# Expert part of a fused GNN and mixture-of-experts kernel: W1 held in the array from a fixed buffer, h made transposed, gathers placed behind the scatters

## The chip, the cores and the metric

One core of one Trainium2 chip. The metric is the device time of one execution in microseconds; a kernel's time is the median of its runs.

## The reference, cut to what matters

625 nodes with 256 features pass a three-level edge convolution (20,000 edges) and are added to the input. What follows is the part that the change touches: a layer norm, a gate that picks 2 of 8 experts for each node, and for each picked expert a two-layer network.

```python
gate_scores = x @ Wg + bg
_, idx = jax.lax.top_k(gate_scores, K)                    # K = 2 of E = 8
h = jax.nn.gelu(jnp.einsum('td,edh->teh', xf, W1) + b1[None], approximate=False)   # D = 256, H = 512
y = jnp.einsum('teh,ehd->ted', h, W2) + b2[None]
out = jnp.einsum('ted,te->td', y, mf)                     # sum over the picked experts
x = x + out
```

All of it is float32.

## The kernel before

The convolution takes the first 117 us of the span and is not touched. The expert part works on the picked pairs only. The 1250 (node, expert) pairs are sorted by expert into tiles of 128 slots; each tile belongs to one expert (`owner_i`), and there are at least `FIXED` = 10 tiles and at most 17. The trace has 13: ten in code that is written out, two in one turn of a loop over pairs of tiles (`Fori`), and one behind an `If`. Unused slots are sent to spare rows behind the output.

In what follows tile s is counted from 0. For each tile:

- its x rows: tiles 0 and 1 are gathered by one-hot matmuls (`gather` on PE, lines 1529 to 1540); from tile 2 on by an indirect DMA of POOL from `x2_rows` in DRAM (`gather`, line 587) into one of twelve buffers `xg`, then transposed on PE (`transpose_x`, line 1552) and copied by ACT to `xt` (line 787, tiles 0 and 1: line 799);
- `up` (line 1545): for each half k of the 256 features, the transposed x is the stationary operand and 512 columns of W1 move; two float32 matmuls, which the trace shows as four instructions. h comes out with slots on partitions;
- DVE adds b1 (line 1203), ACT applies gelu (line 792), PE transposes h in four pieces (line 1558), ACT copies them to `h_t` (line 796);
- `down` (line 1564): four float32 matmuls (eight instructions) with a piece of `h_t` held and 256 columns of W2 moving;
- DVE adds b2 and writes y to one of four buffers `y_sb` (line 1207);
- POOL adds the rows of y to the output in DRAM with an accumulating indirect DMA (`scatter`, line 593).

A node has two experts, so two scatters can hit the same output row. POOL therefore waits for `scattered`, that is for the landing of scatter s - 1, before it issues scatter s. POOL's queue is in this order: the gathers of tiles 2 to 9, then for s = 0 to 9 scatter s and, for s below 4, the gather of tile 10 + s. In the loop it waits for the landing, copies the row numbers of the tile to a fixed column (`row_put`, line 613), waits for that copy, counts `pool_turn` up (line 616), scatters, copies the next fetch's row numbers (`row_get`, line 624), counts up again and gathers.

PE's order in step s is: transpose h of tile s, up of tile s + 1, transpose x of tile s + 2, down of tile s. Ahead of the expert tiles PE runs filler matmuls on the identity (`keep_busy`, line 1272: float32, 128 columns held, 128 moving; each shows as two instructions).

SP loads b1 as eight broadcasts to 128 partitions and b2 as one (lines 479 to 482), behind the copy of x1 to the output; ACT's queue stores the normed rows to `x2_rows` (lines 780 and 781), which POOL's first gather waits for (line 582), as it does for `row_of` (`rows_ready`, line 1231).

Of the kernel before, what the change touches and what calls it, by code (L numbers as in the profile page):

```python
# [8 lines left out]
D = 256  # L9
LEVELS = 3  # L10
EXPERTS = 8
# [73 lines left out]
FIXED = -(-2 * NODES // P)  # L85
assert FIXED % 4 == 2 and SPARE + P <= NPAD + P


def build(nc, x, src, dst, W, B, Wf, bf, Wg, bg, W1, b1, W2, b2, out):
# [8 lines left out]
    with ctx:  # L98
# [83 lines left out]
        b1_bc = sb("b1_bc", [P, EXPERTS, HID], f32, ffn)  # L182
# [48 lines left out]
        h_pre = sb("h_pre", [P, 2, HID], f32, ffn)  # L231
        h_act = sb("h_act", [P, 2, HID], f32, ffn)
        h_t = sb("h_t", [P, HC, P], f32, ffn)
# [105 lines left out]
        pre_ready = sem("pre_ready")  # L339
        act_ready = sem("act_ready")  # L340
        t_done = sem("t_done")
        h_t_ready = sem("h_t_ready")
        down_done = sem("down_done")
# [50 lines left out]
        def first_experts(kind):  # L394

            _, ids = nc.values_load_multi_w_load_instructions(
                owner_i[0:1, 0:FIXED + 1], engines=(kind,), min_val=0, max_val=EXPERTS - 1,
                skip_runtime_bounds_check_because="a count of at most EXPERTS, cut to EXPERTS - 1 just above")
            return ids
# [47 lines left out]
        def _(sp):  # L447
# [31 lines left out]
            for e in range(EXPERTS):  # L479
                sp.dma_start(b1_bc[:, e, :], b1[e].partition_broadcast(P)).then_inc(ffn_b_in, 16)  # L480
# [7 lines left out]
        def _(pool):  # L488
# [121 lines left out]

            def late_scatter(s, h, n_late):
                pool.wait_ge(scattered, s * 16)
                pool.tensor_copy(row_put[:, h:h + 1], row_of[:, ds(s, 1)]).then_inc(put_taken, 1)
                pool.wait_ge(put_taken, n_late)
                pool.wait_ge(y_ready, s + 1)
                pool.sem_inc(pool_turn, 1)
                scatter(2 + h, row_put[:, h:h + 1])

            with pool.Fori(0, more) as p:
# [18 lines left out]
        def _(act):  # L638
# [155 lines left out]
            def h_transposed(s):  # L794
                act.wait_ge(t_done, s + 1)
                act.copy(h_t[:], bank[2].rearrange("p (k s) -> p k s", k=HC)).then_inc(h_t_ready, 1)  # L796
# [3 lines left out]
            gelu(0, 0)  # L800
            gelu(1, 1)
            for s in range(FIXED):
                h_transposed(s)
                x_transposed(s + 2, s % 2)
                if s:
                    gelu(s + 1, (s + 1) % 2)
            act.wait_ge(experts_ready, 2)
            more = pairs(act)
            with act.Fori(0, more) as p:
                for h in range(2):  # L810
                    s = p * 2 + (FIXED + h)
                    h_transposed(s)
                    x_transposed(s + 2, h)
                    gelu(s + 1, 1 - h)
            with act.If(odd_tile(act) > 0):
                h_transposed(more * 2 + FIXED)
# [3 lines left out]
        def _(dve):  # L820
# [366 lines left out]
            dve.tensor_copy(owner_i[:], owner[:])  # L1187
# [13 lines left out]
            def add_b1(s, h, e):  # L1201
                dve.wait_ge(up_done, s + 1)
                dve.tensor_tensor(h_pre[:, h, :], up_bank(h)[:, :], b1_bc[:, ds(e, 1), :], ALU.add).then_inc(pre_ready, 1)  # L1203
# [29 lines left out]
            dve.wait_ge(ffn_b_in, 16 * (EXPERTS + 1))  # L1233
            e_of = first_experts(mybir.EngineType.DVE)
            add_b1(0, 0, e_of[0])
            add_b1(1, 1, e_of[1])
            for s in range(FIXED):
                if s:
# [391 lines left out]
```

## Time and profile before

| | us |
|---|---|
| median of three runs | 209.98 (209.79 to 211.39) |
| profiled execution, its own time | 211.53 |
| its span, first to last instruction | 209.7 |
| expert tiles, first up to the last scatter's start | 138.24 to 202.88 |

The span is what the trace shows; 1.83 us of the profiled execution's time lie outside it. Rows give a start in us from the span's start, a length, the engine and the line. A PE row's length includes the way through the array, so that neighbouring matmuls overlap in the list; their starts tell the pace. An entry in square brackets is the idle time ahead of an instruction and who ended it. The granted clock of TensorE is at its full level from 63 us until the last expert tile's matmuls at about 195 us.

### The profile page before, as it was taken

What the parts mean: (1) busy time and instruction counts of PE and PEld (TensorE: products, weight loads), DVE (VectorE), ACT (ScalarE), POOL (GpSimd) and SP (SyncE); (2) the same over time, 40 slices, a digit from 0 to 9 for tenths busy, and PEclk for the clock granted to TensorE, in tenths of its full rate; (3) what the DMA queues carried; (4) which work ended last, traced back from release to release, by engine and by line L of the source; (5) the groups of instructions that cost most, each with busy time, mean ns of one, the idle gap of its engine ahead of it and who ended that gap; (6) DMA issues with size and microseconds to landing.
All of it is one profiled execution on the core that took longest, in us unless ns stands there. A gap on an engine that the chain in (4) does not pass through costs nothing.

```text
span 209.7 us, 3186 instructions
## 1 busy us (share of the span) xinstructions
PE 163.0 (78%) x1033; PEld 134.7 (64%) x1034; DVE 101.5 (48%) x268; ACT 71.9 (34%) x196; POOL 61.4 (29%) x85
## 2 busy tenths in 40 slices
PE   0351175858999999999999979997999999997100
PEld 0240165647998779998899969965677667665100
DVE  5499699797009465414624878922232223222000
ACT  4283586563004116202520076023334434343000
POOL 7006000000960039003000200027864732243660
PEclk9999999995599999999999999999999999999755
DMA  5500022000014000699990079903344332322332
GB/s 151 166 15 0 0 90 66 0 2 3 2 17 140 3 5 0 157 377 366 366 367 28 18 211 289 367 18 102 102 65 81 54 30 32 41 25 27 53 50 25
DMA packets 16121, 20.50 MB, mean 98 GB/s; under 512 B 1842, under 2 KB 12452, under 8 KB 15972
## 3 DMA queue, kind: packets, MB, share of 16 engines
q1 hardware_dynamic: 12580, 15.75, 23.2%
q0 software_dynamic: 2544, 3.54, 10.3%
q10 hardware_dynamic: 976, 0.93, 1.4%
q8 instruction: 13, 0.21, 0.4%
q14 instruction: 8, 0.07, 0.1%
HBM read 16.96 MB, written 3.26 MB: 96 GB/s over the span
## 4 chain that ended last, share of the span: by engine, by line
PE 45%; DMA 20%; DVE 18%; issue 8%; POOL 3%; ACT 2%; ACTq 1%; POOLq 0%; DVEq 0%
DMA out_rows<-y_sb,row_of 14%; PE bank L1412 5%; DVE hot_lo L874 4%; DMA out_rows<-y_sb,row_put 4%; PE cnt_ps L1412 3%; PE bank L1265 3%; PE cnt_ps L1272 3%; PE bank L1267 3%; PE bank L1266 3%; PE g_ps L1265 3%; DVE hot_key L877 2%; PE g_ps L1266 2%; PE g_ps L1267 2%; DMA dst_chunk<-in_dst 2%; POOL out_rows L593 2%
## 5 line engine op out<-in xcount | busy, mean ns | idle before, releaser
L1564 PE MATMUL cnt_ps<-w_sb,h_t 128*128 x104 | 24.8, 381 | 1.7 <-ACT h_t L796 1.7
L1313 PE MATMUL bank<-hot_key,hot_lo 125*128 125x45 bf16 (+4 forms) x80 | 8.4, 244 | 18.7 <-DVE hot_key L877 9.1
L1564 PEld LDWEIGHTS cnt_ps<-w_sb,h_t 128*128 128x128 f32 x104 | 18.7, 190 | 4.2 <-issue 2.2
L593 POOL DMA_INDIRECT out_rows<-y_sb,row_of x10 | 15.7, 1574 | 18.3 <-DMA out_rows<-y_sb,row_of 13.0
L1313 PEld LDWEIGHTS bank<-hot_key,hot_lo 125*128 125x128 bf16 x80 | 5.4, 123 | 21.5 <-DVE hot_key L877 14.4
L587 POOL DMA_INDIRECT xg<-x_rows,row_of x12 | 11.8, 983 | 22.8 <-DMA x_rows<-x_f 19.4
L1207 DVE TENSOR_TENSOR y_sb<-cnt_ps,b_bc 128x256 f32<-128x256 f32 x13 | 5.5, 424 | 22.8 <-PE cnt_ps L1564 12.0
L874 DVE TENSOR_TENSOR hot_lo<-iota_lo,edge_rel 125x1024 bf16<-125x1024 int16 x20 | 13.6, 681 | 2.1 <-PE g_ps L1313 2.0
L1545 PE MATMUL bank<-w_sb,xt 128*128 x28 | 13.3, 596 | 0.0
L1272 PE MATMUL cnt_ps<-ident 128*128 128x128 f32 x100 | 12.0, 277 | 0.0
L557 POOL IOTA key_tables<- 128x720 int16 x1 | 2.2, 2244 | 32.9 <-DVE a_hi L960 32.9
L796 ACT COPY h_t<-cnt_ps 128x512 f32<-128x512 f32 x13 | 7.6, 585 | 11.8 <-PE cnt_ps L1558 11.8
L1272 PEld LDWEIGHTS cnt_ps<-ident 128*128 128x128 f32 x100 | 11.5, 192 | 0.0
L1545 PE MATMUL g_ps<-w_sb,xt 128*128 x24 | 11.3, 593 | 0.0
L792 ACT ACTIVATE h_act<-h_pre 128x512 f32<-128x512 f32 x13 | 8.2, 630 | 7.6 <-DVE h_pre L1203 7.6
L1412 PE MATMUL bank<-a_hi,ys_hi 128*128 128x384 f32 x30 | 10.2, 341 | 0.5 <-issue 0.5
L1203 DVE TENSOR_TENSOR h_pre<-bank,b_bc 128x512 f32<-128x512 f32 x7 | 4.8, 691 | 11.7 <-PE bank L1545 11.7
L1412 PE MATMUL bank<-a_hi,ys_lo 128*128 128x384 f32 x30 | 10.1, 338 | 0.0
L787 ACT COPY xt<-bank 128x256 f32<-128x256 f32 x12 | 4.5, 372 | 14.9 <-PE bank L1552 14.9
L1265 PE MATMUL g_ps<-w_hi,ht_hi 128*128 128x256 f32 x30 | 9.3, 310 | 0.0
L1266 PE MATMUL g_ps<-w_lo,ht_hi 128*128 128x256 f32 x30 | 9.1, 304 | 0.0
L1267 PE MATMUL g_ps<-w_hi,ht_lo 128*128 128x256 f32 x30 | 9.1, 303 | 0.0
(270 smaller groups left out, 427.9 us busy)
## 6 DMA issues: line engine op xcount, KB each, us to landing
w_sb<-in_L_ffn_W SPq DMA_DIRECT2D x16, 512.0 KB, 9.5
b_bc<-in_L_ffn_b SPq DMA_DIRECT2D x8, 256.0 KB, 5.6
w_stage<-in_L_gnn_W SPq DMA_DIRECT2D x3, 512.0 KB, 4.1
w_stage<-in_L_gnn_Wf SPq DMA_DIRECT2D x4, 256.0 KB, 4.4
b_bc<-in_L_ffn_b SPq DMA_DIRECT2D x1, 1024.0 KB, 12.3
x_rows<-x_f ACTq DMA_DIRECT2D x1, 640.0 KB, 8.4
x_sb<-in_x SPq DMA_DIRECT2D x1, 512.0 KB
out_rows<-x_sb SPq DMA_DIRECT2D x1, 512.0 KB
```

The source lines that it names most:

```text
L587: pool.indirect_dma_start(out=xg[:, b, :], out_offset=None, in_=x2_rows, in_offset=bass.IndirectOffsetOnAxis(ap=rows, axis=0)).then_inc(x_ ...
L593: pool.indirect_dma_start(out=out, out_offset=bass.IndirectOffsetOnAxis(ap=rows, axis=0), in_=y_sb[:, b, :], in_offset=None, compute_op=AL ...
L792: act.activation(h_act[:, h, :], h_pre[:, h, :], ACT.Gelu).then_inc(act_ready, 1)
L874: dve.tensor_tensor(hot_lo[:, u % RING:u % RING + 2, :, :], iota_lo[0:EP].unsqueeze(1).broadcast_to((EP, 2, P, CT)), rel[:, 0].unsqueeze(2 ...
L1265: pe.matmul(out_, lh, rh, start=first, stop=False, skip_group_check=True)
L1266: pe.matmul(out_, lh, rl, start=False, stop=False, skip_group_check=True)
L1267: return pe.matmul(out_, ll, rh, start=False, stop=last, skip_group_check=True)
L1272: pe.matmul(bank[free][:, 0:P], ident[:], ident[:], start=True, stop=True)
L1313: last = pe.matmul(pane(k), hot_lo[:, u % RING, :, i], hot_keys(u)[:, 0, :, i], start=i == i0, stop=i == i0 + n_i - 1, skip_group_check=True)
L1412: step = pe.matmul(z_bank(i), y[:, u, m], a_t[:, u, cols], start=first and u == 0 and y is y_parts[0], stop=last and u == NT - 1 and y is ...
L1545: last = pe.matmul(up_bank(h)[:, :], xt[:, k, h * P:(h + 1) * P], w1_sb[:, ds(e, 1), k, :], start=k == 0, stop=k == KC - 1)
L1564: last = pe.matmul(bank[3][:, 0:D], h_t[:, k, :], w2_sb[:, ds(e, 1), k, :], start=k == 0, stop=k == HC - 1)
```

## The change

- **W1.** Each tile's W1 (256 x 512) and b1 are copied from where all experts lie to one of two fixed buffers, `w1_now` and `b1_now`: for tiles 0 and 1 by ACT ahead of the copy of their x, from tile 2 on by DVE (`take_w1`), one step and more ahead of use.
- **up** holds 128 columns of `w1_now` and moves the 128 columns of x: eight float32 matmuls of 128 columns. h comes out transposed, so that the four transposes on PE, the copy of `h_t` on ACT and the addition of b1 on DVE go. gelu reads PSUM in four pieces, each with its b1 column as bias, and writes `h_t`, which has two buffers now.
- **b1** is loaded once, as 32 rows of 128, transposed on PE behind the filler matmuls and ahead of the gather, and copied by ACT. The eight broadcasts go.
- **PE's order** in step s is: wait for xt of tile s + 1, transpose x of tile s + 2, up of tile s + 1, down of tile s. In step 0 it is down of tile 0, then transpose x of tile 2.
- **POOL's order**: gathers of tiles 2 to 6, then for s = 0 to 9 scatter s and, for s below 7, the gather of tile 7 + s. In the loop the copy to `row_put` for the next scatter stands behind the present one.

```diff
+AHEAD = 7
...
-            for e in range(EXPERTS):
-                sp.dma_start(b1_bc[:, e, :], b1[e].partition_broadcast(P)).then_inc(ffn_b_in, 16)
+            sp.dma_start(b1_rows[:], b1.rearrange("e (c p) -> (e c) p", c=HC)).then_inc(b1_in, 16)
...
-            for s in range(2, FIXED):
+            for s in range(2, AHEAD):
                 gather(s, row_of[:, s:s + 1])
             pool.wait_ge(x1_stored, 48)
             for s in range(FIXED):
+                pool.wait_ge(y_ready, s + 1)
                 if s:
                     pool.wait_ge(scattered, s * 16)
-                pool.wait_ge(y_ready, s + 1)
                 scatter(s % 4, row_of[:, s:s + 1])
-                if s < 4:
-                    gather((FIXED + s) % (FIXED + 2), row_of[:, FIXED + s:FIXED + s + 1])
+                if AHEAD + s < FIXED + 4:
+                    gather((AHEAD + s) % (FIXED + 2), row_of[:, AHEAD + s:AHEAD + s + 1])
...
+            def next_put(s, h):
+                pool.tensor_copy(row_put[:, h:h + 1], row_of[:, ds(s, 1)]).then_inc(put_taken, 1)
             def late_scatter(s, h, n_late):
-                pool.wait_ge(scattered, s * 16)
-                pool.tensor_copy(row_put[:, h:h + 1], row_of[:, ds(s, 1)]).then_inc(put_taken, 1)
                 pool.wait_ge(put_taken, n_late)
                 pool.wait_ge(y_ready, s + 1)
+                pool.wait_ge(scattered, s * 16)
                 pool.sem_inc(pool_turn, 1)
                 scatter(2 + h, row_put[:, h:h + 1])
...
                     late_scatter(s, h, p * 2 + (h + 1))
+                    next_put(s + 1, 1 - h)
                     pool.wait_ge(x_t_done, s + 1)
...
             def gelu(s, h):
-                act.wait_ge(pre_ready, s + 1)
-                act.activation(h_act[:, h, :], h_pre[:, h, :], ACT.Gelu).then_inc(act_ready, 1)
+                act.wait_ge(up_done, s + 1)
+                act.wait_ge(w1_now_ready, s + 1)
+                for c in range(HC):
+                    last = act.activation(h_t[:, h, c, :], up_bank(h)[:, c * P:(c + 1) * P], ACT.Gelu,
+                                          bias=b1_now[:, h, c:c + 1])
+                last.then_inc(h_t_ready, 1)
+            act.wait_ge(b1_t_ps, 1)
+            act.copy(b1_t[:], bank[2][:, 0:EXPERTS * HC].rearrange("p (e c) -> p e c", e=EXPERTS))\
+                .then_inc(b1_t_ready, 1)
+            act.wait_ge(b1_t_ready, 1)
+            act.wait_ge(owner_ready, 1)
+            e_of = first_experts(mybir.EngineType.Activation, 2)
+            for h in range(2):
+                act.copy(b1_now[:, h, :], b1_t[:, ds(e_of[h], 1), :])
+                act.copy(w1_now[:, h, :, :], w1_sb[:, ds(e_of[h], 1), :, :]).then_inc(w1_now_ready, 1)
             act.wait_ge(gathered, 1)
             act.copy(xt[:], gather_ps()).then_inc(xt_ready, 2)
             gelu(0, 0)
+            x_transposed(2, 0)
             gelu(1, 1)
-            for s in range(FIXED):
-                h_transposed(s)
+            for s in range(1, FIXED):
                 x_transposed(s + 2, s % 2)
-                if s:
-                    gelu(s + 1, (s + 1) % 2)
+                gelu(s + 1, (s + 1) % 2)
...
+            def take_w1(s, h, e):
+                dve.wait_ge(up_done, s - 1)
+                dve.wait_ge(h_t_ready, s - 1)
+                dve.tensor_copy(b1_now[:, h, :], b1_t[:, ds(e, 1), :])
+                dve.tensor_copy(w1_now[:, h, :, :], w1_sb[:, ds(e, 1), :, :]).then_inc(w1_now_ready, 1)
...
             for s in range(FIXED):
-                if s:
-                    dve.wait_ge(act_ready, s)
-                    add_b1(s + 1, (s + 1) % 2, e_of[s + 1])
+                take_w1(s + 2, s % 2, e_of[s + 2])
                 if s >= 4:
                     dve.wait_ge(scattered, 16 * (s - 3))
                 add_b2(s, s % 4, e_of[s])
...
-            def up(s, h, e):
+            def up(s, h):
                 pe.wait_ge(xt_ready, s + 1)
-                for k in range(KC):
-                    last = pe.matmul(up_bank(h)[:, :], xt[:, k, h * P:(h + 1) * P], w1_sb[:, ds(e, 1), k, :],
-                                     start=k == 0, stop=k == KC - 1)
+                pe.wait_ge(w1_now_ready, s + 1)
+                for c in range(HC):
+                    for k in range(KC):
+                        last = pe.matmul(up_bank(h)[:, c * P:(c + 1) * P], w1_now[:, h, k, c * P:(c + 1) * P],
+                                         xt[:, k, h * P:(h + 1) * P], start=k == 0, stop=k == KC - 1)
                 last.then_inc(up_done, 1)
...
             keep_busy(WARM_GATHER)
+            pe.wait_ge(b1_in, 16)
+            pe.transpose(bank[2][:, 0:EXPERTS * HC], b1_rows[:], ident[0:EXPERTS * HC, 0:EXPERTS * HC])\
+                .then_inc(b1_t_ps, 1)
             pe.wait_ge(x2_lo_done, NT)
             gather()
...
+            up(0, 0)
+            up(1, 1)
+            down(0, 0, e_of[0])
+            transpose_x(2, 1)
+            for s in range(1, FIXED):
+                pe.wait_ge(xt_ready, s + 2)
                 transpose_x((s + 2) % (FIXED + 2), 1)
-                if s:
-                    pe.wait_ge(y_ready, s)
-                down(s, e_of[s])
+                pe.wait_ge(h_t_ready, s)
+                up(s + 1, (s + 1) % 2)
+                pe.wait_ge(y_ready, s)
+                down(s, s % 2, e_of[s])
```

The loop and the odd tile are changed in the same way on PE, ACT and DVE.

## Rows read from the trace of the kernel before

**Rows 1.** The page, part 4: lines on the chain that ended last

```profile
DMA out_rows<-y_sb,row_of 14%; PE bank L1412 5%; DVE hot_lo L874 4%; DMA out_rows<-y_sb,row_put 4%; PE cnt_ps L1412 3%; PE bank L1265 3%; PE cnt_ps L1272 3%; PE bank L1267 3%; PE bank L1266 3%; PE g_ps L1265 3%; DVE hot_key L877 2%; PE g_ps L1266 2%; PE g_ps L1267 2%; DMA dst_chunk<-in_dst 2%; POOL out_rows L593 2%
```

**Rows 2.** Timeline, POOL alone, 134 to 210 us: start, length, line, [idle before <-releaser]

```profile
140.18 1.19 POOL L587 DMA_INDIRECT xg<-x_rows,row_of  x1 [19.43 <-DMA x_rows<-x_f]
...
145.44 0.94 POOL L587 DMA_INDIRECT xg<-x_rows,row_of  x1 [0.30 <-issue]
...
149.19 0.95 POOL L587 DMA_INDIRECT xg<-x_rows,row_of  x1 [0.30 <-issue]
150.44 1.63 POOL L593 DMA_INDIRECT out_rows<-y_sb,row_of  x1 [0.30 <-issue]
...
187.80 1.55 POOL L593 DMA_INDIRECT out_rows<-y_sb,row_of  x1 [2.46 <-DMA out_rows<-y_sb,row_of]
...
192.82 1.56 POOL L593 DMA_INDIRECT out_rows<-y_sb,row_put  x1 [0.88 <-DVE y_sb L1207]
...
195.43 1.03 POOL L587 DMA_INDIRECT xg<-x_rows,row_get  x1 [0.83 <-POOL row_get L624]
...
202.88 1.58 POOL L593 DMA_INDIRECT out_rows<-y_sb,row_put  x1 [0.88 <-POOL row_put L613]
```

**Rows 3.** The chain of waits in order of time: start, length, what

```profile
150.44 3.72 DMA out_rows<-y_sb,row_of
154.16 0.27 issue
...
171.31 4.15 issue
...
192.07 0.55 issue
```

**Rows 4.** Timeline, all engines, one tile: start, length, engine, line

```profile
154.04 0.60 PE L1558 MATMUL cnt_ps<-ident,h_act 128*128 128x128 f32 x4
...
154.47 1.88 PE L1545 MATMUL bank<-w_sb,xt 128*128 x4
...
156.41 1.89 PE L1564 MATMUL cnt_ps<-w_sb,h_t 128*128 x8
...
158.14 0.60 PE L1558 MATMUL cnt_ps<-ident,h_act 128*128 128x128 f32 x4
```

**Rows 5.** Timeline, from the gathered tiles to y of tile 0

```profile
137.46 0.59 ACT L799 COPY xt<-bank 128x512 f32<-128x512 f32 x1 [6.74 <-PE bank L1538]
...
138.24 1.96 PE L1545 MATMUL bank<-w_sb,xt 128*128 x4
...
138.69 0.18 DVE L1231 SCALAR_TENSOR_TENSOR row_of<-bank,unused 128x20 int32<-128x20 f32 x1
...
144.03 1.96 PE L1564 MATMUL cnt_ps<-w_sb,h_t 128*128 x8 [0.47 <-ACT h_t L796]
...
146.14 0.43 DVE L1207 TENSOR_TENSOR y_sb<-cnt_ps,b_bc 128x256 f32<-128x256 f32 x1 [3.39 <-PE cnt_ps L1564]
```

**Rows 6.** Timeline, the filler matmuls ahead of the gather

```profile
129.41 5.60 PE L1272 MATMUL cnt_ps<-ident 128*128 128x128 f32 x48
```

**Rows 7.** Groups by line and shape, ScalarE: busy, mean ns of one

```profile
L689 ACT CAST w_hi<-w_stage 128x512 fp32r<-128x512 f32 x3 | 1.7, 615 | 5.4 <-DVE w_stage L913 5.4
...
L678 ACT COPY a_f<-g_ps 128x95 f32 x4 | 1.0, 242 | 0.0
```

**Rows 8.** Line 389: a register load of one value, ns min/median/max

```profile
L389 ACTq TENSOR_LOAD <-pairs_i x1: 413/413/413, 181.9 to 181.9; - x1
```

**Rows 9.** Line 781, the second store of x_rows: us from issue to landing

```profile
DMA to landing us min/median/max: 10.8/10.8/10.8
```

**Rows 10.** The page, part 6: the b1 loads, KB each, us to landing

```profile
b_bc<-in_L_ffn_b SPq DMA_DIRECT2D x8, 256.0 KB, 5.6
```

**Rows 11.** Groups by line and shape, VectorE: busy, mean ns of one

```profile
L874 DVE TENSOR_TENSOR hot_lo<-iota_lo,edge_rel 125x1024 bf16<-125x1024 int16 x20 | 13.6, 681 | 2.1 <-PE g_ps L1313 2.0
...
L1216 DVE TENSOR_TENSOR hot_place<-iota_p,pos_f 128x1280 fp32r<-128x1280 f32 x1 | 1.5, 1481 | 0.0
```

More of the change, by code:

```diff
@@ L338, in build @@
         up_done = sem("up_done")
-        pre_ready = sem("pre_ready")
-        act_ready = sem("act_ready")
-        t_done = sem("t_done")
         h_t_ready = sem("h_t_ready")
+        b1_in = sem("b1_in")
+        b1_t_ps = sem("b1_t_ps")
+        b1_t_ready = sem("b1_t_ready")
+        owner_ready = sem("owner_ready")
+        w1_now_ready = sem("w1_now_ready")
         down_done = sem("down_done")
@@ L392, in odd_tile, with first_experts @@
             return eng.value_load(pairs_i[0:1, 1:2], min_val=0, max_val=1)
-        def first_experts(kind):
+        def first_experts(kind, n):
             _, ids = nc.values_load_multi_w_load_instructions(
-                owner_i[0:1, 0:FIXED + 1], engines=(kind,), min_val=0, max_val=EXPERTS - 1,
+                owner_i[0:1, 0:n], engines=(kind,), min_val=0, max_val=EXPERTS - 1,
                 skip_runtime_bounds_check_because="a count of at most EXPERTS, cut to EXPERTS - 1 just above")
@@ L1186, in _ @@
             mark(dve.scalar_tensor_tensor(in_tile[:], from_tile[:], float(P), from_tile[:], ALU.is_le, ALU.mult))
[L1187 removed]
+            dve.tensor_copy(owner_i[:], owner[:]).then_inc(owner_ready, 1)
             wait_marked()
@@ L1232, in _ @@
             dve.wait_ge(experts_ready, 2)
[L1233 to L1236, printed above, removed]
+            dve.wait_ge(ffn_b_in, 16)
+            e_of = first_experts(mybir.EngineType.DVE, FIXED + 2)
+            dve.wait_ge(b1_t_ready, 1)
             for s in range(FIXED):
-                if s:
-                    dve.wait_ge(act_ready, s)
-                    add_b1(s + 1, (s + 1) % 2, e_of[s + 1])
+                take_w1(s + 2, s % 2, e_of[s + 2])
                 if s >= 4:
@@ L1247, in _ @@
                     s = p * 2 + (FIXED + h)
-                    e_up = expert_of(dve, s + 1)
+                    e_up = expert_of(dve, s + 2)
                     e_down = expert_of(dve, s)
-                    dve.wait_ge(act_ready, s)
-                    add_b1(s + 1, 1 - h, e_up)
+                    take_w1(s + 2, h, e_up)
                     dve.wait_ge(scattered, s * 16 - 16)
@@ L1553, in transpose_x, with down @@
                 last.then_inc(x_t_done, 1)
-            def transpose_h(s, h):
-                pe.wait_ge(act_ready, s + 1)
-                for k in range(HC):
-                    last = pe.transpose(bank[2][:, k * P:(k + 1) * P], h_act[:, h, k * P:(k + 1) * P], ident[:])
-                last.then_inc(t_done, 1)
-            def down(s, e):
+            def down(s, h, e):
                 pe.wait_ge(h_t_ready, s + 1)
                 for k in range(HC):
-                    last = pe.matmul(bank[3][:, 0:D], h_t[:, k, :], w2_sb[:, ds(e, 1), k, :], start=k == 0,
+                    last = pe.matmul(bank[3][:, 0:D], h_t[:, h, k, :], w2_sb[:, ds(e, 1), k, :], start=k == 0,
                                      stop=k == HC - 1)
@@ L1578, in _ @@
             pe.wait_ge(experts_ready, 2)
[L1579 to L1585 removed]
+            e_of = first_experts(mybir.EngineType.PE, FIXED)
+            up(0, 0)
[4 more added lines that the diff above has]
+                pe.wait_ge(xt_ready, s + 2)
                 transpose_x((s + 2) % (FIXED + 2), 1)
[L1587 to L1589 removed]
+                pe.wait_ge(h_t_ready, s)
+                up(s + 1, (s + 1) % 2)
+                pe.wait_ge(y_ready, s)
+                down(s, s % 2, e_of[s])
             more = pairs(pe)
```

37 lines of the change are left out of this document (11 added, 26 removed).

## The prediction

> **What bounds the kernel now.** I read the chain that ended last first. Its largest part is the landing of scatters, 14% and 4% of the span [rows 1]; all of PE's `up` and `down` together do not appear among its leading lines. Then POOL's own timeline [rows 2]: eight gathers from 140.18, and right behind them scatter 0 at 150.44. From there scatters follow one another: 3.72 us from the start of a scatter to its landing, 0.27 until the next one starts [rows 3]. Ten scatters from 150.44 to 187.80 are 9 intervals of 37.36 us, 4.15 on average (one of them 4.9, with a late landing [rows 3]); then three in the loop and the `If`, at 192.82 and 202.88 the first and last, 5.0 apart [rows 2]. Behind the last start come 6.82 us to the span's end. So the end is the start of scatter 0, plus nine intervals, plus three long ones, plus 6.82.
>
> Then the same stretch on PE [rows 4]: PE is full, one tile from 154.04 to 158.14, 4.10 us. The two pipelines run at nearly the same pace, but y of tile 0 is ready at 146.57 [rows 5], four microseconds before its scatter, and this lead is kept. PE is busy without being the bound; POOL's queue is. A change is worth what it does to the start of the scatter chain and to its intervals.
>
> **The steady tile.** PE loses the four transposes of h, 0.43 (154.04 to 154.47, with the pace of the next instruction) and gets the new `up`. The old one takes 4 instructions of 512 columns: 156.41 less 154.47 is 1.94, of which two transposes of x take about 0.23 (half of the four of h), so 1.71. The new one is 16 instructions of 128 columns with a load each. That shape is in the trace: the filler on the identity, 48 in 5.60 us, 0.117 each with the loads beside it [rows 6], so 16 x 0.117 = 1.87. `down` stays, 158.14 less 156.41 = 1.73. A tile costs PE 0.23 + 1.87 + 1.73 = 3.83 in place of 4.10. Since the scatters need 4.0 to 4.15 a tile, these 0.27 become slack and buy nothing at the end. For PE to become the bound it would have to lose 0.3 a tile.
>
> ACT and DVE have the room: ACT goes from three pieces a tile to the copy of x and four short gelus (at about 0.3 each, below), DVE from one addition of 512 columns to a copy of 1024. w1 of tile s + 2 is copied right behind y of tile s - 1, and used one step later, so PE doesn't see it. `take_w1` waits for gelu of tile s, and behind it on DVE stands only b2 of tile s, which is needed two microseconds later. The ring of four y buffers doesn't bind: y leads the scatter by little more than one tile. The gathers behind scatters stand in the 2.1 us in which POOL only waits for a landing; scatters 0 to 3 had one already, at intervals no longer than the later ones. Gather 7 starts at 148 and tile 7 is transposed near 160.
>
> **The start: POOL's side.** Three gathers fewer ahead of scatter 0: 149.19 to 150.44 is one, 1.25, so 3.75. The first gather now starts at 140.18; `row_of` is ready at 138.69 + 0.18 = 138.87 [rows 5]. What came last by the profile is the store of x_rows, which took 10.8 us to land [rows 9], beside eight b1 broadcasts of 256 KB [rows 10]. These 2 MB go, and the store should land well before 138. Then the first gather waits for `row_of`: 138.87 + 0.1 for the b1 transpose that now stands on PE ahead of it + 0.27 from release to start [rows 3] = 139.25, 0.9 earlier. The bounds of this are 0 and 0.93; I take the whole. Five gathers: the fifth starts 5.26 behind the first, the next instruction 1.25 later [rows 2]; scatter 0 could start at 139.25 + 6.51 = 145.8.
>
> **The start: y's side.** Now ACT has work ahead of the copy of x. The b1 transpose can't run before the filler's end at 135.0 [rows 6], so: copy of b1 0.24 (like 95 columns, 0.242 [rows 7]), register load 0.41 for one value [rows 8] plus its decoding, about 0.75 for two, then two rounds of a short copy of 0.2 and one of 1024 columns. 512 columns take 0.615 and 95 take 0.242 [rows 7], 0.9 ns a column, so about 1.05. 135.1 + 0.24 + 0.75 + 2.5 = 138.6, where the copy of x had started at 137.46 [rows 5]: 1.1 us late. up of tile 0 starts at 139.35 in place of 138.24; up 0 and up 1 are 3.74, so down of tile 0 can start at 143.1. gelu of tile 0 is four pieces of 0.24 (PSUM, 95 columns) to 0.35, 1.2 in all, from 141.4 to 142.6: hidden behind up 1. Before, down had to wait for b1, gelu, transpose and copy, and started at 144.03; y was ready 2.54 later. Now y is ready at 145.6, and scatter 0 starts at 145.8: both sides meet. One stall is new: in step 1 PE waits for the copy of tile 2's x right behind its transpose, about 0.9 with latency and the copy's 0.4. y of tile 1: 143.1 + 1.73 + 0.9 + 3.83 + 0.17 + 0.45 = 150.2, so scatter 1 starts at 150.3 and not at 145.8 + 3.99 = 149.8. From y of tile 2 on (154.0 against 154.3) the chain of landings leads. Before, scatter 1 started at 154.43, so the chain is **4.1 us** earlier (3.7 if the first gather doesn't move).
>
> **The late scatters.** Before, each had between landing and start: 0.2 for addresses, the copy to `row_put` 0.19, and 0.7 to 0.85 behind the count of `pool_turn` (0.55 of it the row of [rows 3]), 1.24 in all. The copy and its wait move behind the previous scatter; the count stays. I take 0.85, a gain of 0.4 for each. In the loop another thing comes near: a gather ended 3.64 behind its scatter's start (195.43 + 1.03 against 192.82 [rows 2]), and with one more copy of about 0.2 ahead of it 3.85, as late as the landing. So 0.4, 0.35 and 0.4, **1.15** in all. Bounds: 0 (the count and the fuller queue eat it) and 2.0 (only 0.27 remains, and POOL's queue binds in the loop).
>
> **Sum.** 4.1 + 1.15 = 5.25 us off the profiled execution of 211.53, and since everything outside the stretch is the same, off the median: 209.98 - 5.25 = **204.7**. Around it: 3.7 + 0 gives 206.3, 4.1 + 2.0 gives 203.9, and 0.6 more where the late landing (4.9 for 4.1) doesn't come again, 203.3.
>
> **Rivals.** *First: DVE's copy holds POOL up.* DVE now copies 1024 float32 columns from SBUF to SBUF in each tile, and it starts right behind y, that is at the very time at which POOL makes a scatter's descriptors (1.57 us in each interval). The rows before show POOL's scatters at 1.55 to 1.63 whether DVE adds beside them or rests [rows 2], but those additions read PSUM; no copy of this kind is there. If such a copy stops POOL while it runs, with L its length, a scatter is delayed by L if the copy falls into it and by L/2 if it starts inside a copy: (1.57 L + L²/2) / 4.05 for random phases. DVE's 1024 columns took 0.68 at 16 bits, and 1280 of float32 took 1.48, which gives 1.22 for 1024 [rows 11]. With 0.68 the price is 0.32 a scatter, 4.2 for 13, 208.9; with 1.22 it is 0.66, 8.5, **213.2**, slower than before. It turns slower where a scatter pays over 0.4, a copy of about 0.83. The upper end needs the plain rate and a complete stop. Gathers that it hits have slack, so I set its middle at 208. Chance 0.26.
>
> The Trainium skill (SBUF — State Buffer, Who interferes with whom) says just that: a float32 copy inside SBUF runs in a mode that takes the ports which DVE shares with GpSimd, and descriptor generation stands still until the copy ends. Its page VectorE: DVE Perf Modes (The perf-mode tier table) gives such a copy twice the plain rate; an estimate from its 1227 ns for 2048 columns is 0.69 us for 1024. By that rule the low end of this rival holds; no row of the trace before can show it.
>
> *Second: only the queue's order pays.* The first gather doesn't move (3.7 in place of 4.1) and the late turns keep their 5.0: 206.3. For it: nothing in the trace shows what 0.55 us behind the count are. Chance 0.13.
>
> *Third: the loads aren't hidden.* If each of up's 16 loads (0.19) stood alone because their addresses change, up would take 3.04, a tile 5.0, and y of tile 12 would come at 206, 213. Against it: [rows 6] has the same load before each matmul at 0.117. Chance 0.03.
>
> **How the numbers follow.** Forecast 0.58 (203.3 to 206.3), then 0.26, 0.13 and 0.03. The range is 203.2 to 208.7, which leaves out the upper part of the first rival and the third. One per cent, 2.1 us, is about what a measurement can tell here: faster is the forecast, the second rival and a part of the first (0.07), 0.78; within 1% most of the rest of it, 0.13; slower 0.09.
>
> **What would show it.** Right: first gather near 139.3, scatter 0 near 145.8 with five gathers ahead, intervals of 4.0 to 4.15, late ones of 4.6, PE at 3.8 a tile with growing lead of y over the scatters, 16 instructions of `up` at 0.117. The first rival shows as scatters longer than 1.6 us, or landings over 3.85, where a copy of DVE lies beside them. Wrong would be: y of tile 0 later than 146, intervals that follow y, or a first gather that still starts behind 140.

## The result, and the profile after

| | before | after |
|---|---|---|
| median, us | 209.88 (209.62 to 211.39, 4 runs) | 212.44 (211.68 to 212.83, 4 runs) |
| profiled execution | 211.53 | 212.52 |
| its span | 209.7 | 210.3 |

The ratio is 1.010, 95% interval 1.006 to 1.014: about 1% slower, where 204.7 us were forecast. Some executions of any of these kernels take over 1.5% longer than its fastest; medians are over all runs, ratios and intervals leave those out. POOL's timeline of the changed kernel, with the columns of [rows 2]:

```profile
140.96 1.19 POOL L590 DMA_INDIRECT xg<-x_rows,row_of  x1 [19.79 <-issue]
...
146.44 0.95 POOL L590 DMA_INDIRECT xg<-x_rows,row_of  x1 [0.30 <-issue]
147.69 1.71 POOL L596 DMA_INDIRECT out_rows<-y_sb,row_of  x1 [0.30 <-issue]
...
152.41 1.59 POOL L596 DMA_INDIRECT out_rows<-y_sb,row_of  x1 [1.50 <-DMA out_rows<-y_sb,row_of]
...
189.67 1.93 POOL L596 DMA_INDIRECT out_rows<-y_sb,row_of  x1 [3.07 <-DVE y_sb L1224]
...
194.52 1.57 POOL L596 DMA_INDIRECT out_rows<-y_sb,row_put  x1 [2.72 <-DVE y_sb L1224]
...
199.06 1.57 POOL L596 DMA_INDIRECT out_rows<-y_sb,row_put  x1 [0.78 <-DMA out_rows<-y_sb,row_put]
...
203.64 1.56 POOL L596 DMA_INDIRECT out_rows<-y_sb,row_put  x1 [0.82 <-DMA out_rows<-y_sb,row_put]
```

(The profile names DVE as the releaser of the scatter at 189.67, but y of tile 9 had been ready for 9.6 us by then; what came last was the landing of scatter 8, at 188.92 in the chain.)

Scatter 0 is 2.75 us earlier than before, and the last one 0.76 later. What lies between can be read from the rows alone: 189.67 less 147.69 is 41.98 us for nine intervals, 4.66 each, against 37.36 and 4.15 in [rows 2]. The chain of waits says what each interval gained. Its first three lines are the first gather's:

```profile
139.67 0.03 issue
139.70 0.02 POOLq L586
139.71 1.24 issue
...
165.64 0.03 issue
165.67 0.02 POOLq L606
165.68 0.75 issue
166.43 3.76 DMA out_rows<-y_sb,row_of
170.19 0.02 issue
```

In [rows 3] 0.27 us lie between a landing and the next scatter. Here it is 0.02, then an instruction of 0.02 on POOL's queue, line 606, then 0.75. Line 606 is `pool.wait_ge(scattered, s * 16)`. The line's own view:

```profile
L606 POOLq EVENT_SEMAPHORE  x9: 17/17/17, 151.6 to 188.9; - x9
```

The wait for the landing has become an instruction of its own (a lone wait, in what follows), nine times. In the kernel before it left no record; there the wait for y (line 603) had one, and it passed microseconds ahead of time. The edit that swaps the two waits stands in the diff; in the changed kernel the landing is the later of the two each time.

The conv part ahead is unchanged, but the first filler matmul starts at another time in each trace, from 127.45 to 130.98 us over fifteen traces. So most times below are counted from the start of the row `x48` of the fillers ([rows 6], 129.41 before, 129.82 after):

| us behind the fillers' start | before | after |
|---|---|---|
| `row_of` ready | 9.46 | 9.84 |
| first gather of POOL | 10.77 | 11.14 |
| y of tile 0 | 17.16 | 15.53 |
| scatter 0 | 21.03 | 17.87 |
| scatter 9 | 58.39 | 59.85 |
| last scatter | 73.47 | 73.82 |

From one event to the next: first gather +0.37, gathers -3.53, nine intervals +4.62, late scatters -1.11; sum +0.35. The 1.0 us between the profiled executions is these 0.35, 0.41 of the fillers' start and 0.2 behind the last scatter's start and outside the span. The medians are 2.6 apart; the experiments come back to that.

PE and DVE do in a tile what was forecast. A tile of the changed kernel on PE, with its DVE rows:

```profile
153.12 0.38 PE L1567 MATMUL bank<-ident,xg 128*128 128x128 f32 x2
...
153.34 1.95 PE L1560 MATMUL bank<-xt,w_now 128*128 128x128 f32 x16
153.43 0.42 DVE L1224 TENSOR_TENSOR y_sb<-cnt_ps,b_bc 128x256 f32<-128x256 f32 x1 [2.64 <-PE cnt_ps L1573]
...
153.84 0.69 DVE L1220 COPY w_now<-w_sb 128x1024 f32 x1
...
155.13 1.89 PE L1573 MATMUL cnt_ps<-w_sb,h_t 128*128 x8
...
156.86 0.38 PE L1567 MATMUL bank<-ident,xg 128*128 128x128 f32 x2
```

3.74 us a tile (153.12 to 156.86), and 1.79 from the start of `up` (L1560) to that of `down` (L1573): 0.112 for each of the 16 instructions with its load. The copy of W1 takes 0.69 here.

### The profile page after: what moved, and what is told of

Its sections match the earlier page's. It is cut to its first block, busy times and chain, and to the rows that moved or that the text cites. A ratio compares the mean times of both kernels' runs of the same rounds, so it can differ in the third digit from the quotient of the medians.

```text
span 210.3 us, 3448 instructions
## 1 busy us (share of the span) xinstructions
PE 161.5 (77%) x1138; PEld 145.2 (69%) x1139; DVE 101.4 (48%) x279; ACT 73.2 (35%) x227; POOL 63.6 (30%) x85
## 4 chain that ended last, share of the span: by engine, by line
PE 50%; DMA 19%; DVE 18%; issue 6%; POOL 3%; ACT 1%; ACTq 1%; POOLq 0%; DVEq 0%
DMA out_rows<-y_sb,row_of 13%; PE bank L1425 5%; DVE hot_lo L888 4%; PE cnt_ps L1425 3%; PE cnt_ps L1573 3%; PE bank L1278 3%; PE cnt_ps L1285 3%; PE bank L1280 3%; PE bank L1279 3%; PE g_ps L1278 3%; PE g_ps L1280 2%; DVE hot_key L891 2%; PE g_ps L1279 2%; DMA dst_chunk<-in_dst 2%; DMA out_rows<-y_sb,row_put 2%
## 5 line engine op out<-in xcount | busy, mean ns | idle before, releaser
L1573 PE MATMUL cnt_ps<-w_sb,h_t 128*128 x104 | 27.7, 414 | 7.0 <-DVE y_sb L1224 4.5
L1573 PEld LDWEIGHTS cnt_ps<-w_sb,h_t 128*128 128x128 f32 x104 | 20.4, 207 | 10.5 <-issue 7.9
L596 POOL DMA_INDIRECT out_rows<-y_sb,row_of x10 | 16.7, 1672 | 17.5 <-DMA out_rows<-y_sb,row_of 10.7
L590 POOL DMA_INDIRECT xg<-x_rows,row_of x12 | 13.1, 1090 | 23.1 <-issue 23.1
L1560 PE MATMUL bank<-xt,w_now 128*128 128x128 f32 x112 | 13.8, 276 | 0.0
L1560 PEld LDWEIGHTS bank<-xt,w_now 128*128 128x128 f32 x112 | 13.1, 192 | 0.1
L1560 PE MATMUL g_ps<-xt,w_now 128*128 128x128 f32 x96 | 11.7, 275 | 0.0
L802 ACT ACTIVATE h_t<-bank,b_now 128x128 f32<-128x128 f32 x28 | 8.0, 369 | 10.4 <-PE bank L1560 10.4
L1560 PEld LDWEIGHTS g_ps<-xt,w_now 128*128 128x128 f32 x96 | 11.2, 192 | 0.0
L802 ACT ACTIVATE h_t<-g_ps,b_now 128x128 f32<-128x128 f32 x24 | 6.9, 370 | 7.1 <-PE g_ps L1560 7.1
```

The costliest lines, as they stand in the source:

```text
L590: pool.indirect_dma_start(out=xg[:, b, :], out_offset=None, in_=x2_rows, in_offset=bass.IndirectOffsetOnAxis(ap=rows, axis=0)).then_inc(x_ ...
L596: pool.indirect_dma_start(out=out, out_offset=bass.IndirectOffsetOnAxis(ap=rows, axis=0), in_=y_sb[:, b, :], in_offset=None, compute_op=AL ...
L802: last = act.activation(h_t[:, h, c, :], up_bank(h)[:, c * P:(c + 1) * P], ACT.Gelu, bias=b1_now[:, h, c:c + 1])
L1560: last = pe.matmul(up_bank(h)[:, c * P:(c + 1) * P], w1_now[:, h, k, c * P:(c + 1) * P], xt[:, k, h * P:(h + 1) * P], start=k == 0, stop=k ...
L1573: last = pe.matmul(bank[3][:, 0:D], h_t[:, h, k, :], w2_sb[:, ds(e, 1), k, :], start=k == 0, stop=k == HC - 1)
```

## The experiments

Every kernel's trace is given by the same marks, in us behind the fillers' start. The second number in the column of the first gather is its distance from `row_of`. "Nine" is scatter 0 to scatter 9, "late" from there to the last scatter. y 0 is y of tile 0.

| kernel | first gather | y 0 | scatter 0 | nine | late | last | median, us |
|---|---|---|---|---|---|---|---|
| before | 10.77 (1.31) | 17.16 | 21.03 | 37.36 | 15.08 | 73.47 | 209.88 |
| after | 11.14 (1.30) | 15.53 | 17.87 | 41.98 | 13.97 | 73.82 | 212.44 |
| a_wait_old | 11.15 (1.31) | 15.53 | 17.87 | 37.92 | 13.58 | 69.37 | 208.15 |
| b_wait_new | 10.77 (1.30) | 17.16 | 21.05 | 41.33 | 15.13 | 77.51 | 216.44 |
| b_queue_only | 10.76 (1.30) | 17.15 | 18.02 | 36.90 | 15.03 | 69.95 | 208.57 |
| a_no_copy | 11.15 (1.31) | 15.52 | 17.67 | 38.04 | 13.69 | 69.40 | 206.10 |
| a_two_copies | 11.12 (1.28) | 15.52 | 17.90 | 38.39 | 13.47 | 69.76 | 208.33 |
| a_gather_wait | 10.14 (0.30) | 15.52 | 16.64 | 37.26 | 13.48 | 67.38 | 205.54 |
| a_b1_early | 10.77 (1.28) | 14.97 | 17.31 | 37.78 | 13.89 | 68.98 | 206.34 |
| b_queue_gather | 10.32 (0.85) | 17.16 | 18.02 | 36.91 | 14.38 | 69.31 | 207.84 |
| a_old_queue | 11.14 (1.30) | 15.52 | 22.03 | 38.05 | 15.01 | 75.09 | 212.71 |
| a_best7 | 9.79 (0.30) | 14.96 | 16.74 | 38.19 | 13.68 | 68.61 | 206.61 |
| a_best5 | 9.79 (0.30) | 14.97 | 15.83 | 37.48 | 14.17 | 67.48 | 206.42 |

The medians of the experiments come from three sets, each on a chip of its own: a_wait_old, b_wait_new, b_queue_only and a_no_copy with the kernel before at 210.94 beside them; a_two_copies, a_gather_wait, a_b1_early and b_queue_gather with it at 210.16; a_old_queue, a_best7 and a_best5 with it at 211.70. The ratios below are each to the kernel before on the same chip.

**a_wait_old.** The swap undone in the changed kernel:

```diff
-                pool.wait_ge(y_ready, s + 1)
                 if s:
                     pool.wait_ge(scattered, s * 16)
+                pool.wait_ge(y_ready, s + 1)
                 scatter(s % 4, row_of[:, s:s + 1])
```

> The changed kernel with one edit: in the ten written-out tiles POOL waits for the last scatter's landing first and for y second, as before the change. Theory A (order of the two waits): the wait written last stands as an instruction of its own, and a scatter behind it starts 0.77 us after the landing in place of 0.27; the nine intervals go from 4.66 back to about 4.15, 4.4 us less, so 208.0. Rival B (DVE's copy of W1 holds POOL's descriptor work up): the order does nothing, intervals stay near 4.66, 212.4. Rival C (seven gathers behind scatters instead of four lengthen the intervals): intervals with a gather stay at 4.6, no change either.

Ratio 0.982 (0.970 to 0.993). Nine intervals fall from 41.98 to 37.92, 4.06 of the 4.4 expected, and the last scatter from 73.82 to 69.37. The chain of its trace has the old gap again, and no instruction in it:

```profile
164.44 0.27 issue
164.71 3.83 DMA out_rows<-y_sb,row_of
168.54 0.27 issue
```

Theory A holds. Rival C falls, since the seven gathers are all still behind scatters, and so does rival B as the cause of these 4 us, since DVE still copies W1.

**b_wait_new.** The same swap, alone, in the kernel before.

```diff
+                pool.wait_ge(y_ready, s + 1)
                 if s:
                     pool.wait_ge(scattered, s * 16)
-                pool.wait_ge(y_ready, s + 1)
```

> The kernel before with one edit: POOL waits for y first and for the last scatter's landing second. Theory A: start to start goes from 4.15 to 4.6 for nine scatters, 4.3 us slower than before, 214.2. Rivals B and C: nothing else of the change is in it, so 209.9.

Ratio 1.026 (1.018 to 1.033), the nine intervals 41.33. Here nothing else of the change is in the kernel:

```profile
180.45 0.02 issue
180.48 0.02 POOLq L603
180.50 0.71 issue
181.21 3.78 DMA out_rows<-y_sb,row_of
```

0.75 from landing to start, 4.0 us for nine. The swap costs 4 us, in both directions.

**b_queue_only.** POOL's part of the change in the kernel before, without the swap: `AHEAD = 7`, gathers behind seven scatters, `next_put`.

```diff
-            for s in range(2, FIXED):
+            for s in range(2, AHEAD):
                 gather(s, row_of[:, s:s + 1])
...
-                if s < 4:
-                    gather((FIXED + s) % (FIXED + 2), row_of[:, FIXED + s:FIXED + s + 1])
+                if AHEAD + s < FIXED + 4:
+                    gather((AHEAD + s) % (FIXED + 2), row_of[:, AHEAD + s:AHEAD + s + 1])
...
```

> The kernel before with POOL's part of the change alone: five gathers ahead of scatter 0, seven behind scatters, row_put copied early in the loop; the order of the two waits stays that of before. Theory A: scatter 0 starts 3.5 earlier (near 146.9, when y of tile 0 is there), intervals stay at 4.1, the three late ones lose 0.4 each: 209.9 - 3.5 - 1.1 = 205.3. Rival C (the gathers behind scatters cost): intervals of 4.6 where a gather lies between, 3.3 us for seven, 208.6. Rival B says as theory A here, since DVE copies nothing.

Ratio 0.986 (0.972 to 0.999). Scatter 0 is 3.0 earlier and waits for y of tile 0 (ready at 17.15); intervals are 4.10 with seven gathers between them, so rival C falls here too. The late part shows the gain in two intervals (4.53 and 4.67 against 5.02 and 5.07) and lost it in the third, 5.83 with a late landing. The last scatter is 3.5 earlier where 4.6 were expected, and the late landing alone is 1.2. So POOL's part of the diff gives 3.5 us in the last scatter's start, where the changed kernel with its faults mended gives 4.9 (a_best7, below).

The bound has moved in this kernel. y of tile 1 to 9 is ready only 0.76 to 0.90 before its scatter starts, and a start about 0.8 behind the lone wait's signal is what such a wait takes (line 604; 0.76 in the rows below). The chain that ended last runs through PE's tiles, 4.10 each, up to y of tile 9:

```profile
180.88 1.74 PE cnt_ps L1570 x8
...
182.82 0.44 DVE y_sb L1213
183.26 0.03 issue
183.28 0.02 POOLq L604
183.30 0.49 issue
183.79 0.22 POOLq L390
184.01 3.74 DMA out_rows<-y_sb,row_of
```

With the queue mended, PE and the landings set nearly the same pace.

**a_no_copy** and **a_two_copies** change the amount of copying on DVE, on top of a_wait_old. In a_no_copy the tiles from 2 on compute with the W1 of tiles 0 and 1.

```diff
 # a_no_copy
-                dve.tensor_copy(b1_now[:, h, :], b1_t[:, ds(e, 1), :])
-                dve.tensor_copy(w1_now[:, h, :, :], w1_sb[:, ds(e, 1), :, :]).then_inc(w1_now_ready, 1)
+                dve.tensor_copy(b1_now[:, h, :], b1_t[:, ds(e, 1), :]).then_inc(w1_now_ready, 1)
 # a_two_copies
                 dve.tensor_copy(b1_now[:, h, :], b1_t[:, ds(e, 1), :])
+                dve.tensor_copy(w1_extra[:, h, :, :], w1_sb[:, ds(e, 1), :, :])
                 dve.tensor_copy(w1_now[:, h, :, :], w1_sb[:, ds(e, 1), :, :]).then_inc(w1_now_ready, 1)
```

> As a_wait_old, but DVE doesn't copy W1 from tile 2 on (these tiles compute with the W1 of tiles 0 and 1; only b1 is copied). Theory A with little of B: the lengthened scatters (1.92 us at two places, 1.68 to 1.72 at two more, in the changed kernel) all become 1.55 to 1.63, about 0.9 us less than a_wait_old. Rival B in full strength: 0.3 to 0.66 for each scatter, 4 us or more less than a_wait_old.

> As a_wait_old, but DVE copies each tile's W1 twice, first to a buffer that nobody reads: 1.38 us of copy a tile in place of 0.69. If a copy stops POOL whenever it meets descriptor work, the scatters' lengths show it: about 0.33 a scatter at 0.69 and 0.8 at 1.38 for random phases, so 4 us slower than a_wait_old. If it costs only the 0.1 to 0.2 us that single scatters of a_wait_old show over 1.58 (0.6 in sum), 0.5 to 1.5 us slower.

The lengths of the 13 scatters tell it. Without the copy all are 1.55 to 1.63. With one, four of a_wait_old's are longer, by 0.1 to 0.2; the sum over 1.58 a scatter is 0.56 there, 0.89 in the changed kernel and 0.39 to 0.94 over the eight traces with one copy. With two copies it is 1.09. In the timeline of a_two_copies the longest one stands beside both copies:

```profile
166.80 0.69 DVE L1221 COPY w_extra<-w_sb 128x1024 f32 x1
166.91 2.04 POOL L597 DMA_INDIRECT out_rows<-y_sb,row_of  x1 [1.11 <-DVE y_sb L1226]
167.41 0.69 DVE L1222 COPY w_now<-w_sb 128x1024 f32 x1
```

At 166.91, right behind a copy's start, a scatter takes 2.04 in place of 1.58. The cost goes when the copy goes, so DVE's copy does hold POOL up, as the rival said; but it is 0.03 to 0.07 a scatter with one copy, not the 0.32 to 0.66 of my formula. That two copies cost more isn't shown, since 1.09 in one trace lies close above 0.94.

How much a scatter loses goes by when the copy starts, counted from the scatter's start. These are all 43 scatters that meet a copy in the eight traces with one copy a tile:

| copy's start, us from the scatter's start | scatters | scatter longer by, us |
|---|---|---|
| -0.56 to -0.55 | 4 | 0.13 |
| -0.35 to -0.13 | 6 | 0.21 to 0.44, more the later the copy ends |
| -0.03 to 0.55 | 9 | 0.00 to 0.05 |
| 0.56 to 0.94 | 9 | 0.09 to 0.14 |
| 0.97 to 1.17 | 8 | 0.16 to 0.37, more the later it starts |
| 1.31 to 1.58 | 7 | 0.00 to 0.01 |

The changed kernel has a scatter at 157.03 that took 1.59 with a copy 0.55 behind its start, and one at 161.60 that took 1.92, 0.22 behind a copy's. A scatter that starts inside a copy is held up until about 0.1 before the copy's end. Waiting goes the other way too: the six copies that start 0.56 to 0.80 behind a scatter's start took 0.79 to 1.02 in place of 0.69.

The last scatters don't show the cost (69.40 without a copy, 69.37 with one, 69.76 with two), because single late events are as large: a_no_copy has 4.90 between scatters 0 and 1, where y of tile 1 came late, and 4.88 between 2 and 3. The ratios are 0.976 (0.969 to 0.983) for a_no_copy and 0.993 (0.988 to 0.998) for a_two_copies, on two chips, with a_wait_old's 0.982 (0.970 to 0.993) overlapping both.

**a_gather_wait.** a_wait_old with the waits ahead of the first gather swapped.

```diff
-            pool.wait_ge(x2_stored, 32)
             pool.wait_ge(rows_ready, 1)
+            pool.wait_ge(x2_stored, 32)
```

> As a_wait_old, and ahead of POOL's first gather the wait for the row numbers comes first and the wait for the stored rows second. Theory (the wait written last stands alone and costs): first gather 0.5 to 0.75 earlier behind row_of (1.24 to 1.3 us before), the chain with it, 0.5 us or a little less off a_wait_old. Rival (the 1.3 us are a first DMA's own start): no change, 208.

Ratio 0.981 (0.976 to 0.986). In the changed kernel the later of two signals had stood alone here too. Now the wait for `row_of` leaves no record:

```profile
138.94 0.19 DVE row_of L1248
139.13 0.29 issue
139.42 1.18 POOL xg L590
```

0.29 from `row_of` to the first gather where the changed kernel has 0.03 + 0.02 + 1.24. Twice the gain expected: ahead of this first gather the lone wait costs 1.0, and everything behind it moves, scatter 0 from 17.87 to 16.64 (0.2 of it because no gather ahead of it is lengthened beside a copy). The rival falls.

**a_b1_early.** a_wait_old with b1's transpose ahead of the fillers, in a bank of its own, from which ACT's copy then reads.

```diff
-            keep_busy(WARM_GATHER)
             pe.wait_ge(b1_in, 16)
-            pe.transpose(bank[2][:, 0:EXPERTS * HC], b1_rows[:], ident[0:EXPERTS * HC, 0:EXPERTS * HC])\
+            pe.transpose(g_ps[0][:, 0:EXPERTS * HC], b1_rows[:], ident[0:EXPERTS * HC, 0:EXPERTS * HC])\
                 .then_inc(b1_t_ps, 1)
+            keep_busy(WARM_GATHER)
```

> As a_wait_old, but b1 is transposed ahead of the filler matmuls (into another bank), so that it neither delays the gather nor starts ACT's copies late. Expected: the one-hot gather's first matmul follows the fillers as before the change (5.33 us behind their first and not 5.71), row_of and POOL's chain 0.35 earlier; xt of tiles 0 and 1 about 1.1 earlier, y of tile 0 with it, which POOL doesn't need: 0.35 us off a_wait_old. Rival (y of the first tiles leads the chain): 1 us off.

Ratio 0.986 (0.980 to 0.991). `row_of` comes at 9.49 in place of 9.84, as before the change, and y of tile 0 at 14.97 in place of 15.53, 0.35 and 0.56 (0.35 and 1.1 expected). The last scatter is 0.39 earlier. One transpose of 32 columns costs 0.35 where it stands between a full PE and its next work.

**b_queue_gather.** b_queue_only with the first gather's waits swapped.

> b_queue_only with the waits ahead of the first gather swapped too. The first gather starts 0.5 earlier if the order theory holds there, but scatter 0 waited for y in b_queue_only (147.11 against a queue ready at 146.35), so nothing at the end: as b_queue_only.

Ratio 0.989 (0.980 to 0.997). The first gather comes 0.44 earlier and no more, 0.85 behind `row_of`:

```profile
L584 POOLq EVENT_SEMAPHORE  x1: 17/17/17, 138.7 to 138.7; - x1
...
138.92 0.18 DVE L1237 SCALAR_TENSOR_TENSOR row_of<-bank,unused 128x20 int32<-128x20 f32 x1
...
139.95 1.18 POOL L588 DMA_INDIRECT xg<-x_rows,row_of  x1 [20.14 <-DVE row_of L1237]
```

Line 584 is the wait for the store of `x2_rows`, now the lone one. With the eight broadcasts of b1 in the kernel the store takes 11.2 us to land, and this wait passes at 138.7, 0.4 before `row_of` is ready (139.10); the gather starts 1.2 behind it. So the lone wait leads though its signal isn't the last; by 1.24 against 0.29 it would have to pass about 1.0 before the other. Scatter 0 stays at 18.02, on y of tile 0. Here is what the W1 part is worth: in a_gather_wait, with it, y of tile 0 comes at 15.52 in place of 17.16, scatter 0 at 16.64 and the last one at 67.38 in place of 69.31. PE's shorter tile adds nothing to that: the nine intervals are 37.26 there and 36.91 here.

**a_old_queue.** The W1 part alone: the changed kernel with POOL's code as before.

> The changed kernel with all of POOL's code as before the change: eight gathers ahead of scatter 0, four behind scatters, both orders of waits and the late row_put of before. What is left is the W1 part alone. Theory (POOL's chain is the bound, PE's saving of 0.35 a tile is slack): first gather 0.4 later than before (b1's transpose on PE), the rest of the chain the same, plus about 0.6 for scatters that meet DVE's copy: 210.5 to 211, no faster than before. Rival (a faster tile on PE counts): 0.35 x 13, 4 us less than before.

Ratio 1.008 (1.003 to 1.012). PE saves 0.36 a tile and the kernel is slower. Its last scatter is 1.6 later than before: 0.37 at the first gather, 0.63 in the gathers ahead of scatter 0, 0.69 in the nine intervals, where single scatters take 1.68, 2.02 and 1.72. POOL's part of the gathers, with DVE's copies (line 1215) between:

```profile
142.44 1.16 POOL L590 DMA_INDIRECT xg<-x_rows,row_of  x1 [0.30 <-issue]
...
142.79 0.69 DVE L1215 COPY w_now<-w_sb 128x1024 f32 x1
...
143.91 0.95 POOL L590 DMA_INDIRECT xg<-x_rows,row_of  x1 [0.30 <-issue]
...
147.11 0.76 DVE L1215 COPY w_now<-w_sb 128x1024 f32 x1 [0.31 <-issue]
...
147.66 1.03 POOL L590 DMA_INDIRECT xg<-x_rows,row_of  x1 [0.30 <-issue]
...
150.02 0.69 DVE L1215 COPY w_now<-w_sb 128x1024 f32 x1
150.24 1.28 POOL L590 DMA_INDIRECT xg<-x_rows,row_of  x1 [0.30 <-DVE y_sb L1219]
```

Of the four gathers shown, the three that meet a copy take 1.16, 1.03 and 1.28, the one that doesn't 0.95.

**a_best7** and **a_best5.** The changed kernel with all three mends (the order of waits in the scatters, that ahead of the first gather, and b1's transpose ahead of the fillers), with five and with three gathers ahead of scatter 0 (`AHEAD = 7`, `AHEAD = 5`).

> The changed kernel with the three mends together: landing waited for first in the written-out scatters, row numbers waited for first ahead of the first gather, b1 transposed ahead of the fillers. From the fillers' first matmul: first gather at 9.8 (before 10.8), scatter 0 6.5 behind it, last scatter 57.3 behind it; 1.35 us less than a_wait_old in the same state, 204 to 205.

> a_best7 with three gathers ahead of scatter 0 in place of five. With h made transposed and b1 out of the way y of tile 0 should be ready 15.0 us behind the fillers' start, where the queue of a_best7 is ready at 16.3: scatter 0 starts with y, 1.1 earlier, and the chain follows it: about 1.1 us less than a_best7. Rival (y of tile 1, or the gather of tile 5 behind scatter 0, comes too late): scatter 0 earlier, scatter 1 not, no gain.

Ratios 0.979 (0.969 to 0.989) and 0.973 (0.965 to 0.982). a_best7's trace had one interval of 5.1 and its five gathers took 0.45 more than those of a_gather_wait, so it gets no further than a_gather_wait. a_best5 starts its chain as soon as y of tile 0 is there:

```profile
145.53 0.43 DVE y_sb L1224
145.96 0.02 issue
145.98 0.02 POOLq L606
146.00 0.81 issue
146.81 3.90 DMA out_rows<-y_sb,row_of
```

Scatter 0 at 15.83 is 0.9 earlier than in a_best7, and it now has the lone wait of its own: y is the later one there, and its wait stands alone (0.02, then 0.81). Both intervals lie below 1, but a_gather_wait, a_best7 and a_best5 can't be told apart by their times; a_best5's ratio rests on two runs.

**before_again** and **after_again.** Both kernels unedited, for second traces on one chip.

> The kernel before, unedited, for a second trace: the fillers' first matmul moved between 127.8 and 131.0 us in traces of kernels that are the same up to there, and the two traces that I compare explain 1.0 of the 2.6 us between the medians. Expected from the fillers' start: first gather 10.8, scatter 0 21.0, last scatter 72.7 to 73.5, according to whether the one late landing (0.8) of the first trace comes again; the fillers' start itself anywhere in that range.

> The changed kernel, unedited, beside the one before on the same chip. Expected from the fillers' start: first gather 11.1, scatter 0 17.9, nine intervals of 4.6 to 4.7, last scatter 73.8; 0.3 to 1.1 us later than before_again by that count, and slower than before by 1 to 3 us in the medians.

Last scatters at 72.84 and 73.91, 1.07 apart; nine intervals 36.62 and 41.93. The first trace's late landing (4.9) didn't come again, and that is 0.6 of the difference to the 0.35 above. The medians here are 211.26 and 211.95, the ratios to the kernel before 1.003 (0.997 to 1.008) and 1.004 (0.999 to 1.010). So by the traces the changed stretch is 0.4 to 1.1 us longer, and the 2.6 us between the first medians didn't come again: on this chip the change makes no difference that the runs can tell. The start of the fillers alone moves by up to 3.5 us from run to run, and why isn't known.

## Why the prediction was wrong

**The step that failed** is in the part on the steady tile and in what would show it right: that the nine scatter intervals stay at 4.0 to 4.15, with 0.27 from a landing to the next start. The prediction never mentions that the diff swaps `wait_ge(y_ready)` and `wait_ge(scattered)`, and so puts the swap at nothing. It is most of the loss: of the 4.62 us by which the nine intervals grew (41.98 for 37.36), a_wait_old puts 4.06 back, and b_wait_new makes 3.97 by the swap alone. The other 0.56 a_wait_old still has over the kernel before; its trace shows longer scatters beside DVE's copies and a first interval of 4.30 for 3.99, where the forecast had 4.5. The trace of before had a sign of the swap's cost: in the late scatters the landing is followed by a lone instruction, `pool_turn`'s count, and the next DMA starts over 0.7 us behind it (0.55 of it the row in [rows 3]). The prediction used that for the late scatters and didn't carry it over to the others. Why an indirect DMA behind a lone wait starts so late stays open; the runs show that it does, and by how much.

**The start of the gathers** failed too, in two terms. I took `row_of` + 0.27, 0.93 earlier than before; the first gather came 0.37 later. I had read the store of x_rows as what came last before, from the releaser that the profile names [rows 2]. But the lone wait of that kernel, for `row_of`, passed at 138.9, and the gather started 1.24 behind it, while the store, issued at 128.4, landed at 139.2 [rows 9]. The store does land early now (4.7 us after its issue), which gains nothing, because the lone wait for `row_of` costs the same 1.24 in both kernels; a_gather_wait shows the 0.27 that I had assumed (0.29 there). The transpose of b1 cost 0.35 and not 0.1. Together that is 1.3 us.

**Where the 7.7 us are** by which the forecast is off in the median (212.44 for 204.7): the last scatter was to start 5.25 earlier and started 0.35 later, 5.6. Of these about 4.1 are the swap, 1.3 the start of the gathers and 0.2 the gather lengthened beside DVE's first copy. The remaining 2.1 aren't placed by any trace. The second pair of medians is 0.7 apart where the first is 2.6, so most of them may be chance between runs; that isn't shown.

**The gathers ahead of scatter 0** came as worked out: 3.75 for three, 3.53 measured with 0.24 lost beside DVE's first copy. y of tile 0 was ready at 15.53, 0.7 earlier than forecast (145.6 less 129.41), and 2.3 before its scatter: the two sides didn't meet, and POOL's queue led.

**The late scatters** came as worked out: 15.08 to 13.97, 1.11 for 1.15, with the count kept and the gap from 1.2 to 0.8.

**PE's tile** came as worked out (3.74 for 3.83, from 4.10), and so did its worth at the end: nothing in a_old_queue, nor in the intervals of a_gather_wait. The third rival is out: 0.112 with the load.

**The first rival**, DVE's copy, has the right sign and the wrong size. The copy took 0.69, as the Trainium skill's page VectorE: DVE Perf Modes (The perf-mode tier table) gives by the estimate from its figure for twice the length. (The other length, 1.22, is 1.18 in proportion to its row; nothing hangs on it now.) The Trainium skill's page SBUF — State Buffer (Who interferes with whom) has descriptor generation stand still while the copy runs. The trace agrees for scatters that start inside a copy, which took up to 2.02 with one copy and are held up almost to its end. It doesn't for a copy that starts in the first 0.55 of a scatter, which costs nothing. My formula charged the whole copy wherever it falls into the scatter's 1.57; that is what was wrong in it, and the mean is 0.07 a scatter in the changed kernel, a fifth of what it gave. The time of this rival, 208.9 to 213.2, holds the result by luck, for the reason is another.

**Taken together**: with the two orders of waits mended and b1 out of the way the forecast's mechanism holds. a_best7 is that kernel: its last scatter comes at 68.61, 4.9 earlier than in the first trace of before (4.2 than in the second), where 5.25 was forecast, and its ratio is 0.979 where 204.7 us would be 0.975.

## What to carry to other kernels

Where an indirect DMA of POOL waits for two signals, the order in which the waits are written is part of the critical path: in these kernels the one written last becomes an instruction of its own and the other leaves no record, and the DMA starts 0.5 us (scatters) to 1.0 us (first gather) later when the lone one leads, each time. Other engines and other instructions were not tried. Read which of the two has a row in the trace, and put the signal that comes last where none is. A lone wait leads even if its signal isn't the last but comes within that time of it.

And cost every line of a diff, those that only change places too. A part that is off the bound (PE here) can be made 9% faster a tile for nothing, while POOL's queue alone was worth 1.4%; and once the queue was mended PE's tiles stood on the chain that ended last (b_queue_only), so look again at what bounds the kernel after each step.

## What was not expected of the hardware

- A lone semaphore wait of 0.02 us was followed by 0.75 us until a scatter's start (0.71 in b_wait_new), 0.81 for a_best5's first one and 1.24 until the first gather; where the signal that came last had the wait without a record, the start came 0.27 to 0.29 behind it.
- The first filler matmul started anywhere from 127.45 to 130.98 us in fifteen traces. Marks counted from it agree to 0.03 us for `row_of` and y of tile 0.
- A DVE copy of 0.69 us holds up a scatter of 1.58 by up to 0.44 or by nothing, according to when it starts; a copy that starts inside a scatter can itself be held up, to 1.02.
- A scatter lands 3.6 to 3.9 us after its start, but single ones, at no fixed place, 0.5 to 1.2 later: before the change behind scatter 5 (4.6), in a_best7 one at 4.8, in b_queue_only behind scatter 10 (5.02). No experiment was made on it.
- Whether the late scatters' gap of 0.8 can be brought to 0.27 as well wasn't tried.
